# A recommender's attention scores: smaller pieces of the score table, placed all through the tile

## The chip, the core and the metric

The kernel runs on one core of one Trainium2 chip. The metric is the device time of one execution in microseconds (us), lower is better. A core has a matrix engine (PE; its weight loads are listed apart as PEld), a vector engine (DVE), a scalar engine (ACT), a general engine (POOL) and a queue that only issues transfers (SP). ACT and POOL issue transfers too. Each engine runs its own instructions in order and waits on semaphores for the others.

## The reference

For each of 2048 users there is a history of 200 items. An item is three ids below 1000, each with an embedding of 32 numbers; `ub` holds the histories' embeddings, `q` the embedding of the user's candidate item.

```python
att_in = jnp.concatenate([q, ub, q - ub, q * ub], axis=-1)
h = att_in @ w_att1.T + b_att1
score = (h @ w_att2.T + b_att2)[..., 0]
score = jnp.where(mask, 0.0, score)          # mask: first id is 0
browse = jnp.einsum('bl,ble->be', score, ub)
feat = jnp.concatenate([item_emb, browse, user_emb], axis=-1)
x = _dice(feat @ w1.T + b1, a1, g1, be1)     # normalised over the batch
x = _dice(x @ w2.T + b2, a2, g2, be2)
return jax.nn.sigmoid(x @ w3.T + b3)[:, 0]
```

Both layers in front of the score are linear, so for one user the score of a history item is a sum of three table values, one per id.

## The kernel before

**Work.** The 2048 users are 16 tiles of 128. A tile has 16 steps of 8 users, a step has two slots of 4 users, so a tile has 32 slots. An id is split in a high digit (40 values) and a low digit (25 values).

**Per tile.** PE multiplies the embedding tables with the tile's queries (L568) and gets all 3000 scores of each user. To keep full precision in bf16 the result is split in three parts: ACT copies the first (L761), PE subtracts it (L561), ACT copies the next, and so on. This is the splitting: 7 groups of low digits by 3 parts, one per slot, in slots 7 to 27 of the tile *before* the one that it is for. It writes `scores_b` (score values by table row on the partitions).

**Placement.** `place_scores` (L328) copies `scores_b` to `scoretab` by three transfers, one per id, of 40 partitions each. `scoretab` holds 128 users. The pieces are 16, 16, 32, 32, 32 users. Since the splitting of a tile ends in slot 27, the five pieces go out at its end: piece 0 and 1 in step 14, piece 2 in step 15, pieces 3 and 4 in steps 0 and 1 of the next tile. The next splitting, from slot 7 on, overwrites the one `scores_b`, so ACT waits for all five first (L893).

**Per step n.** DVE compares the high digits with 1 to 40 (`onehot_hi`, L967, for step n + 2), and SP turns the result around by a transposing transfer (`turn_hi`, L324, to `hiT`). In slot s PE multiplies `hiT` with the slot's part of `scoretab` (`read_scores`, L532), which needs the landed transfer and room in `sel` (two slots). DVE reduces `sel` (`pick`, L999) to scores, POOL splits them in three bf16 parts in six small operations (L431 to L444), DVE multiplies them with the one-hot of the low digits (`scale`, L1011), and PE adds them up with `onehot_hi` (`add_scores`, L549), 5 slots behind the reading. ACT copies the sums out (L754) and issues their transfers to `weightsum` (L830).

**DVE's order in a step**: pick(2n), `onehot_hi` of step n + 2, `onehot_lo` (L985), pick(2n + 1), in six steps of a tile a small piece of the digits, then scale(n - 1). `onehot_hi` waits until PE's sums have freed a slot of its ring.

**Unevenly spread work.** PE has the splitting in slots 7 to 27 and "finish" (L637, 25 fp32 products) in slots 9 to 15. POOL issues indirect gathers of item rows in steps 1 and 2 (L409) and of user rows in step 3 (L417). SP issues, in order: the transposes, the placements, a load of ids (`raw`, L315) in steps 2 and 9, and a store in step 11.

**Loops.** DVE, ACT, POOL and SP loop over tiles 1 to 14, one tile per pass. PE's loop holds seven tiles and is passed twice.

**The end.** Behind the last tile two batch-normalised layers run on buffers that reuse `scores_b` and `scoretab` (`x1`, `gate1`, `norm1`).

## Time and profile before

| | |
|---|---|
| median of 3 runs | 1591.98 us (1587.96 to 1605.28) |
| the profiled execution | 1586.62 us, span 1584.8 us |
| DVE busy | 1438.4 us (91%) |
| PE busy | 1328.5 us (84%) |
| POOL busy | 1131.4 us (71%) |
| ACT busy | 717.1 us (45%) |
| TensorE clock granted, mean | 0.921 |
| moved by DMA | 194.21 MB, mean 123 GB/s |

The profile is of one execution. Busy time is the union of an engine's instructions; waits are gaps on an engine, put down to the instruction or transfer whose semaphore came last. Line numbers (L532) are those of the kernel before. Transfers are issued by an engine's queue (SPq, ACTq) and are carried by 16 DMA engines that all queues share; q1 holds what SP issues, q10 what ACT issues, q8 and q14 fetch instructions.

### The profile page before, as it was taken

The page shows a single profiled execution, that of the slowest core. Times are in us where ns is not written, and L with a number is a line of the kernel's source. Part 1 is how long each engine was busy: PE and PEld are TensorE (multiplying, and loading weights), DVE is VectorE, ACT ScalarE, POOL GpSimd, SP SyncE. Part 2 cuts the span into 40 slices and gives each one's busy share as a digit, 9 for nine tenths or more (in the row PEclk, how much of TensorE's full clock was granted, in tenths as well). Part 3 has the DMA queues.
Part 4 walks back from the last instruction along what each step waited for, and adds up shares of the span by engine and source line. Part 5 has one row for each costly group of instructions (what it writes and reads, how often), then busy time and mean ns, then how long its engine had stood idle before and what let it go on. Part 6 is the DMA issues. An engine that isn't in the chain of part 4 may idle for free.

```text
span 1584.8 us, 67332 instructions
## 1 busy us (share of the span) xinstructions
PE 1328.5 (84%) x26911; PEld 1224.4 (77%) x26911; DVE 1438.4 (91%) x1453; ACT 717.1 (45%) x1633; POOL 1131.4 (71%) x1669
## 2 busy tenths in 40 slices
PE   5687989889797988979788797888989798887965
PEld 4576878778796887869788797888879797787861
DVE  7799999999999898999989899898999999899955
ACT  5353544536354453525435353453535355352217
POOL 3588788787878787776766768587787878677830
PEclk8799999999899998999999899999999899898966
DMA  2778676675857686584676758567686856668730
GB/s 30 146 109 159 104 146 124 130 149 111 168 100 151 108 137 134 111 167 95 138 111 128 147 111 154 92 141 131 111 167 112 151 107 144 118 115 157 117 70 0
DMA packets 510281, 194.21 MB, mean 123 GB/s; under 512 B 484005, under 2 KB 491797, under 8 KB 510045
## 3 DMA queue, kind: packets, MB, share of 16 engines
q1 hardware_dynamic: 492454, 162.61, 57.2%
q10 hardware_dynamic: 15448, 26.51, 6.5%
q8 instruction: 221, 3.62, 0.9%
q0 software_dynamic: 2144, 1.36, 0.8%
q14 instruction: 14, 0.11, 0.0%
HBM read 8.45 MB, written 1.44 MB: 6 GB/s over the span
## 4 chain that ended last, share of the span: by engine, by line
POOL 58%; issue 24%; DVE 6%; PE 5%; DMA 2%; POOLq 2%; SPq 2%; ACT 1%; DVEq 0%; ACTq 0%
POOL score L431 16%; POOL score L436 13%; POOL score_r L440 10%; POOL parts L441 6%; POOL parts L444 6%; POOL parts L437 3%; POOL item_rows L409 2%; DMA hiT<-onehot_hi 2%; POOL user_rows L417 2%; PE sel L532 1%; DVE score_j L999 1%; DVE onehot_hi L967 1%; DVE scaled_lo L1011 1%; PE wsum_ps L549 1%; PE misc L637 1%
## 5 line engine op out<-in xcount | busy, mean ns | idle before, releaser
L532 PE MATMUL sel<-scoretab,hiT 128*128 128x75 bf16 x12288 | 560.3, 206 | 142.8 <-DMA hiT<-onehot_hi 116.8
L532 PEld LDWEIGHTS sel<-scoretab,hiT 128*128 128x128 bf16 x12288 | 521.3, 103 | 204.1 <-issue 147.2
L549 PE MATMUL wsum_ps<-scaled_lo,onehot_hi 100*128 100x75 bf16 x12288 | 554.3, 204 | 73.8 <-DVE scaled_lo L1011 73.7
L549 PEld LDWEIGHTS wsum_ps<-scaled_lo,onehot_hi 100*128 100x128 bf16 x12288 | 509.4, 102 | 89.9 <-DVE scaled_lo L1011 83.8
L1011 DVE TENSOR_TENSOR scaled_lo<-onehot_lo,parts 100x3744 bf16<-100x3744 bf16 x256 | 539.4, 2107 | 24.0 <-POOL parts L444 20.0
L754 ACT ACTIVATE wsum_ring<-wsum_ps 128x300 f32<-128x300 f32 x512 | 215.5, 421 | 674.7 <-PE wsum_ps L549 668.1
L431 POOL TENSOR_TENSOR score<-score_j 100x16 f32<-100x16 f32 x256 | 310.4, 1213 | 293.4 <-DVE score_j L999 292.6
L999 DVE TENSOR_REDUCE score_j<-sel 100x24 f32<-100x600 f32 x512 | 395.8, 773 | 34.7 <-PE sel L532 34.0
L967 DVE TENSOR_TENSOR onehot_hi<-digits,iota_hi 100x1920 bf16<-100x1920 bf16 x256 | 297.5, 1162 | 45.9 <-PE wsum_ps L549 45.4
L761 ACT ACTIVATE scores_b<-acc 128x512 bf16<-128x512 f32 (+1 forms) x318 | 256.1, 805 | 44.9 <-PE acc L568 23.7
L436 POOL TENSOR_TENSOR score<-score,score_j 100x16 f32<-100x16 f32 x256 | 229.7, 897 | 22.0
L985 DVE TENSOR_TENSOR onehot_lo<-digits,iota_lo 100x1248 bf16<-100x1248 bf16 x256 | 211.5, 826 | 0.0
L440 POOL TENSOR_TENSOR score_r<-score,parts 100x16 f32<-100x16 f32 x256 | 168.8, 659 | 20.0
L444 POOL TENSOR_TENSOR parts<-score_r,parts 100x32 bf16<-100x32 f32 x256 | 122.8, 480 | 20.1
L441 POOL TENSOR_TENSOR parts<-score,parts 100x32 bf16<-100x32 f32 x256 | 129.2, 505 | 0.0
L637 PE MATMUL misc<-weightsum,table_blk 128*96 128x128 f32 x800 | 113.4, 285 | 4.6 <-DMA weightsum<-wsum_ring 4.6
L568 PE MATMUL acc<-queryT,tableT 97*128 97x128 f32 x758 | 111.6, 289 | 0.0
L561 PE MATMUL acc<-scores_b,minus_identb 128*128 128x512 bf16 (+1 forms) x212 | 101.2, 477 | 0.1
L637 PEld LDWEIGHTS misc<-weightsum,table_blk 128*96 128x96 f32 x800 | 93.9, 168 | 4.8 <-issue 4.8
L409 POOL DMA_INDIRECT item_rows<-in_L_rec_table_i_dram,ids_now x51 | 81.6, 1599 | 20.5 <-POOL ids_now L403 12.5
L568 PEld LDWEIGHTS acc<-queryT,tableT 97*128 97x128 f32 x758 | 94.6, 194 | 0.0
L857 ACT ACTIVATE onehot_hi<-digits,centre 100x48 bf16<-100x48 bf16 x256 | 91.6, 358 | 0.0
(155 smaller groups left out, 663.5 us busy)
## 6 DMA issues: line engine op xcount, KB each, us to landing
scoretab<-scores_b SPq DMA_DIRECT2D x144, 187.5 KB
weightsum<-wsum_ring ACTq DMA_DIRECT2D x128, 125.0 KB
weightsum<-wsum_ring ACTq DMA_DIRECT2D x64, 150.0 KB
scoretab<-scores_b SPq DMA_DIRECT2D x96, 93.8 KB
raw<-in_r_rec_his_dram SPq DMA_DIRECT2D x32, 150.0 KB
hiT<-onehot_hi SPq DMA_TRANSPOSE x256, 4.5
x_rows<-x_tile SPq DMA_DIRECT2D x14, 100.0 KB
scores_b<-x_rows SPq DMA_DIRECT2D x1, 1400.0 KB
```

The source lines that it names most:

```text
L431: pool.tensor_tensor(score_2[:, :], score_j[:, p2, :, 0], score_j[:, p2, :, 1], ALU.add).then_inc(parts_step, 1)
L436: pool.tensor_tensor(score[:, :], score_2[:, :], third, ALU.add)
L440: pool.tensor_tensor(score_r[:, :], score[:, :], parts[:, p2, :, 0, 0], ALU.subtract)
L441: pool.tensor_tensor(parts[:, p2, :, 1, :], twice(score[:, :]), parts[:, p2, :, 0, :], ALU.subtract).then_inc(parts_step, 1)
L444: pool.tensor_tensor(parts[:, p2, :, 2, :], twice(score_r[:, :]), parts[:, p2, :, 1, :], ALU.subtract).then_inc(parts_ready, 1)
L532: mm = pe.matmul(sel[:, 2 * (s % 2) + q, (c % 4) * W:(c % 4 + 1) * W] .rearrange("p (j v) -> p j v", j=NF), hiT[0:HJ, s // 2 % 4, g * POSP ...
L549: mm = pe.matmul(wsum_ps[:, s % 2, b * W:(b + 1) * W].rearrange("p (j v) -> p j v", j=NF), hi_columns(ring_slot(n), g), scaled_lo[:, n % 2 ...
L637: mm = pe.matmul(misc[0:E, 0:TILE].rearrange("p (w b) -> p w b", w=4), table_blk[:, lo, :, :].rearrange("p j e -> p (j e)"), weightsum[0:H ...
L761: act.activation(scores_b[:, :, stage, slice(*ROUNDS[r])], split_bank(first, r), ACT.Copy).then_inc(split_copied, 1)
L967: dve.tensor_tensor(onehot_hi[0:POS, ring_slot(n), :, HB:].rearrange("p g (j v d) -> p g j v d", j=NF, d=2), digits[:, hb, 1, g0:g0 + PER, ...
L999: dve.tensor_reduce(score_j[:, n % 2, g0:g0 + 8, :].rearrange("p (q c) j -> p q (c j)", q=2), sel[0:POS, 2 * (s % 2):2 * (s % 2) + 2, 0:4 ...
L1011: ins = dve.tensor_tensor(scaled_lo[:, n % 2, :, :, :].rearrange("p q i (u d) -> p (q i) u d", d=2), onehot_lo[:, n % 2, :, :, :].rearrang ...
```

## The change

`scoretab` now holds 64 users in four parts of 16 (HELD, CHUNK). Each tile has eight pieces of 16 users instead of five of 16 or 32. Pieces 0 and 1 go out in steps 14 and 15 of the tile before, pieces 2 to 7 behind the transpose of steps 0, 2, 4, 6, 8 and 10. A piece waits until PE has read the slots of the piece four before it (`sel_full`). `scores_b` has two halves that alternate by tile (`odd`), so the splitting of the next tile no longer waits for this tile's placement. The splitting's slots stay.

For `odd` to be a constant, SP and ACT now loop over pairs of tiles, seven passes, and PE has no loop: its 16 tiles are written out. DVE and POOL keep their loops. At the start DVE clears half as much of `scoretab` and copies the same constant rows in 12 smaller pieces instead of 6. At the end `gate1` and `norm1` lie elsewhere.

```diff
+    CHUNK = 16
+    CHUNKS = TILE // CHUNK
+    HELD = 4
...
-        scoretab_flat = sb("scoretab", [128, 2 * NF * HALF * 3 * LO], BF16)
+        scoretab_flat = sb("scoretab", [128, HELD * NF * CHUNK * 3 * LO], BF16)
...
-        scores_flat = sb("scores_b", [HJ, TILE * 3 * LO], BF16)
+        scores_flat = sb("scores_b", [HJ, 2 * TILE * 3 * LO], BF16)
...
-        ROWS = (0, 16, 32, 64, 96, 128)
-        CHUNKS = len(ROWS) - 1
...
-            def place_scores(t, c):
+            def place_scores(t, c, odd):
-                await_ge(split_copied, SPLIT_DONE * (t + 1))
-                b0, b1 = ROWS[c], ROWS[c + 1]
-                if isinstance(t, int) and t == 0:
-                    sp.wait_ge(scoretab_zero, b0 // HALF + 1)
+                g = CHUNKS * t + c
+                if c == 0:
+                    await_ge(split_copied, SPLIT_DONE * (t + 1))
+                if isinstance(g, int) and g < HELD:
+                    sp.wait_ge(scoretab_zero, c // 2 + 1)
                 else:
-                    await_ge(sel_full, SLOTS * t - (SLOTS - b1 // 4))
+                    await_ge(sel_full, (CHUNK // 4) * (g - HELD + 1))
...
-            def tile(t, last=False):
+            def tile(t, odd, last=False):
                 for n in range(STEPS):
-                    if n == 14 and not last:
-                        place_scores(t + 1, 0)
+                    if n >= 14 and not last:
+                        place_scores(t + 1, n - 14, 1 - odd)
                     if n + AHEAD < STEPS:
                         turn_hi(t, n + AHEAD)
                     elif not last:
                         turn_hi(t + 1, n + AHEAD - STEPS)
-                    if n < 2:
-                        place_scores(t, 3 + n)
+                    if n % 2 == 0 and n // 2 + 2 < CHUNKS:
+                        place_scores(t, n // 2 + 2, odd)
                     if n in (2, 9) and not last:
                         load_rows(2 * t + 2 + n // 9)
...
-                    if n >= 14 and not last:
-                        place_scores(t + 1, n - 13)
...
-            with sp.Fori(1, TILES - 1) as t:
-                tile(t)
-            tile(TILES - 1, last=True)
+            with sp.Fori(0, TILES // 2 - 1) as pair:
+                for odd in (1, 0):
+                    tile(pair * 2 + (2 - odd), odd)
+            tile(TILES - 1, 1, last=True)
...
-            with pe.Fori(0, (TILES - 2) // RUN) as run:
-                for i in range(RUN):
-                    for s in range(SLOTS):
-                        slot(run * RUN + (i + 1), s)
+            for t in range(TILES):
+                for s in range(SLOTS):
+                    slot(t, s, t % 2, last=t == TILES - 1)
...
                     if r == 0 and stage == 0:
-                        for c in range(CHUNKS):
-                            act.wait_ge(scoretab_in[c], (t + 1) * (NF * 16))
+                        for q in range(HELD):
+                            act.wait_ge(scoretab_in[q], t * ((CHUNKS // HELD) * (NF * 16)))
...
-            for hb in range(2):
-                dve.memset(scoretab_flat[:, hb * W * 3 * HALF:(hb + 1) * W * 3 * HALF].bitcast(F32), 0.0
-                           ).then_inc(scoretab_clear, 1)
+            half = (HELD // 2) * NF * CHUNK * 3 * LO
+            for h in range(2):
+                dve.memset(scoretab_flat[:, h * half:(h + 1) * half].bitcast(F32), 0.0).then_inc(scoretab_clear, 1)
```

The SP queue at the head of its loop (steps 0 to 2 of a tile), before. ISA and REGISTER_ALU rows are waits and counts; a row x2 is the second and third id of a piece; 40x2400 is a piece of 32 users, 40x1200 one of 16.

```order
L324 DMA_TRANSPOSE hiT<-onehot_hi 128x16x112 [waits sel_full]
L284 ISA
L284 ISA [waits split_copied]
L340 DMA scoretab<-scores_b 40x2400 [waits sel_full]
L340 DMA scoretab<-scores_b 40x2400 x2
L284 REGISTER_ALU
L284 ISA [waits hi_ready,lo_rows_ready]
L324 DMA_TRANSPOSE hiT<-onehot_hi 128x16x112 [waits sel_full]
L340 DMA scoretab<-scores_b 40x2400 [waits split_copied,sel_full]
L340 DMA scoretab<-scores_b 40x2400 x2
```

The same place now:

```order
L324 DMA_TRANSPOSE hiT<-onehot_hi 128x16x112 [waits sel_full]
L284 ISA
L340 DMA scoretab<-scores_b 40x1200 [waits sel_full]
L340 DMA scoretab<-scores_b 40x1200 x2
L284 REGISTER_ALU
L284 ISA [waits hi_ready,lo_rows_ready]
L324 DMA_TRANSPOSE hiT<-onehot_hi 128x16x112 [waits sel_full]
L284 REGISTER_ALU
L284 ISA [waits hi_ready,lo_rows_ready]
L324 DMA_TRANSPOSE hiT<-onehot_hi 128x16x112 [waits sel_full]
```

Between the transposes of step 0 and step 1 a piece of 32 users has become one of 16, and the piece between those of step 1 and step 2 is gone. The next piece stands behind the third transpose, ahead of the load of ids.

The SP queue at the end of a tile (step 15), before:

```order
L284 REGISTER_ALU [waits split_copied]
L340 DMA scoretab<-scores_b 40x1200 [waits sel_full]
L340 DMA scoretab<-scores_b 40x1200 x2
L284 REGISTER_ALU
L284 ISA [waits hi_ready,lo_rows_ready]
L324 DMA_TRANSPOSE hiT<-onehot_hi 128x16x112 [waits sel_full]
L284 REGISTER_ALU [waits split_copied]
L340 DMA scoretab<-scores_b 40x2400 [waits sel_full]
L340 DMA scoretab<-scores_b 40x2400 x2
```

And now, from the same piece on to the jump of the loop:

```order
L284 ISA
L340 DMA scoretab<-scores_b 40x1200 [waits sel_full]
L340 DMA scoretab<-scores_b 40x1200 x2
L284 REGISTER_ALU
L284 ISA [waits hi_ready,lo_rows_ready]
L324 DMA_TRANSPOSE hiT<-onehot_hi 128x16x112 [waits sel_full]
L375 REGISTER_ALU
L375 COMPARE_AND_BRANCH
```

The piece of 32 users behind the last transpose of the tile is gone. Between its two jump instructions SP's loop has 75 rows before and 166 now; ACT's loop has 207 rows before and 412 now, as its pass covers two tiles.

DVE at the start, before:

```order
L1085 MEMSET scoretab 128x7200 x2
L1091 COPY scoretab<-far 8x64x25 [waits scoretab_clear,far_in]
L1091 COPY scoretab<-far 8x64x25 x5
L967 TENSOR_TENSOR onehot_hi<-digits,iota_hi 100x16x120 [waits task_copied,const_ready]
L967 TENSOR_TENSOR onehot_hi<-digits,iota_hi 100x16x120
```

And now:

```order
L1084 MEMSET scoretab 128x3600 x2
L1090 COPY scoretab<-far 8x16x25 [waits scoretab_clear,far_in]
L1090 COPY scoretab<-far 8x16x25 x11
L965 TENSOR_TENSOR onehot_hi<-digits,iota_hi 100x16x120 [waits task_copied,const_ready]
L965 TENSOR_TENSOR onehot_hi<-digits,iota_hi 100x16x120
```

The first `onehot_hi` still stands behind the clearing, which is half as long.

## Rows read from the trace of the kernel before

**Rows 1.** the page: span, then busy time (share of the span) and instructions

```profile
span 1584.8 us, 67332 instructions
...
PE 1328.5 (84%) x26911; PEld 1224.4 (77%) x26911; DVE 1438.4 (91%) x1453; ACT 717.1 (45%) x1633; POOL 1131.4 (71%) x1669
```

**Rows 2.** ACT L798, once per tile: duration, first and last start

```profile
L798 ACT ACTIVATE item_prev<-item_last x14: 309/310/311, 136.5 to 1338.5; 96x128 f32<-96x128 f32 x14
```

**Rows 3.** waits of DVE, 139.7 to 1435.7 us: total, times, longest

```profile
DVE onehot_hi L967 <- PE wsum_ps L549: 42.8, 53, 1.3
DVE score_j L999 <- PE sel L532: 19.4, 14, 2.5
DVE scaled_lo L1011 <- POOL parts L444: 18.4, 30, 1.1
```

**Rows 4.** waits of PE, the same stretch

```profile
PE sel L532 <- DMA hiT<-onehot_hi: 98.8, 72, 4.7
```

**Rows 5.** busy time in two tiles: us, each engine, PEclk, DMA share, GB/s

```profile
230.70:320.80 90.10, 81.04 (x1718) 75.75 (x1716) 86.44 (x88) 44.51 (x105) 71.99 (x103) 0.95 0.67 134
877.80:972.00 94.20, 82.52 (x1715) 76.82 (x1712) 86.52 (x87) 44.10 (x104) 67.81 (x103) 0.93 0.66 127
```

**Rows 6.** DVE in tile 2: busy, mean ns | idle before <-releasers

```profile
L1011 DVE TENSOR_TENSOR scaled_lo<-onehot_lo,parts 100x3744 bf16<-100x3744 bf16 x17 | 35.8, 2107 | 2.7 <-POOL parts L444 2.7
...
L967 DVE TENSOR_TENSOR onehot_hi<-digits,iota_hi 100x1920 bf16<-100x1920 bf16 x16 | 18.6, 1165 | 1.0 <-PE wsum_ps L549 1.0
```

**Rows 7.** DVE by line in tile 9

```profile
L1011 DVE TENSOR_TENSOR scaled_lo<-onehot_lo,parts 100x3744 bf16<-100x3744 bf16 x17 | 35.8, 2108 | 0.9 <-POOL parts L444 0.6 <-PE wsum_ps L549 0.3
L999 DVE TENSOR_REDUCE score_j<-sel 100x24 f32<-100x600 f32 x32 | 24.7, 773 | 2.5 <-PE sel L532 2.5
L967 DVE TENSOR_TENSOR onehot_hi<-digits,iota_hi 100x1920 bf16<-100x1920 bf16 x16 | 18.6, 1161 | 4.3 <-PE wsum_ps L549 4.3
```

**Rows 8.** timeline of the SP queue, around tile 9: start us, us, what xcount

```profile
871.42 2.27 SPq L340 DMA_DIRECT2D scoretab<-scores_b  x3
...
885.23 1.58 SPq L324 DMA_TRANSPOSE hiT<-onehot_hi  x1
887.00 3.12 SPq L340 DMA_DIRECT2D scoretab<-scores_b  x3
890.55 3.27 SPq L324 DMA_TRANSPOSE hiT<-onehot_hi  x1
894.20 0.89 SPq L315 DMA_DIRECT2D raw<-in_r_rec_his_dram  x1
```

**Rows 9.** timeline of PE in tile 9: [idle before <-releaser]

```profile
900.27 1.70 PE L532 MATMUL sel<-scoretab,hiT 128*128 128x75 bf16 x24 [4.58 <-DMA hiT<-onehot_hi]
```

**Rows 10.** busy time at a tile boundary and in the steps behind

```profile
868.00:894.00 26.00, 20.88 (x475) 19.84 (x472) 26.00 (x26) 9.38 (x26) 20.65 (x27) 0.87 0.82 183
900.00:930.00 30.00, 29.73 (x524) 27.66 (x525) 23.68 (x25) 13.10 (x31) 15.52 (x33) 0.92 0.40 76
```

**Rows 11.** timeline of POOL in tile 2: a gather of rows

```profile
257.04 2.15 POOL L417 DMA_INDIRECT user_rows<-in_L_rec_table_user_dram,ids_now  x1 [0.81 <-POOL ids_now L414]
```

**Rows 12.** DVE by line, 22 to 42 us

```profile
L1085 DVE MEMSET scoretab<- 128x7200 f32 x2 | 12.1, 6058 | 2.9 <-issue 2.9
```

**Rows 13.** timeline of all engines at the start of the loop

```profile
38.27 2.71 ACT L761 ACTIVATE scores_b<-sel 128x512 bf16<-128x512 f32 x4
...
45.21 5.04 SPq L340 DMA_DIRECT2D scoretab<-scores_b  x6
...
49.76 0.48 PE L532 MATMUL sel<-scoretab,hiT 128*128 128x75 bf16 x5 [12.65 <-DMA scoretab<-scores_b]
```

**Rows 14.** jump of PE (L698): ns min/median/max

```profile
L698 PEldq COMPARE_BRANCH  x2: 83/1988/3893, 777.2 to 1433.0; - x2
```

**Rows 15.** jump of ACT (L913)

```profile
L913 ACTq COMPARE_BRANCH  x14: 44/50/54, 226.9 to 1434.2; - x14
```

**Rows 16.** page part 3, DMA queues: packets, MB, share of 16 engines

```profile
q14 instruction: 14, 0.11, 0.0%
```

More of the change, by code:

```diff
@@ L181, in build @@
         scoretab_clear = sem("scoretab_clear")
-        scoretab_in = [sem(f"scoretab_in{c}") for c in range(5)]
+        scoretab_in = [sem(f"scoretab_in{q}") for q in range(HELD)]
         weightsum_in = sem("weightsum_in")
@@ L553, in add_scores, with split_piece @@
                 mm.then_inc(wsum_full, 1)
-            def split_piece(r, piece, copied, first=False):
+            def split_piece(r, piece, copied, odd, first=False):
                 o = split_bank(first, r)
@@ L560, in split_piece @@
                     await_ge(split_copied, copied)
-                    mm = pe.matmul(o, minus_identb[:, :], scores_b[:, :, piece - 1, l0:l1], start=False,
+                    mm = pe.matmul(o, minus_identb[:, :], scores_b[:, odd, :, piece - 1, l0:l1], start=False,
                                    stop=(piece == 2), skip_group_check=True)
@@ L654, in task, with slot @@
                     mm.then_inc(task_full, 1)
-            def slot(t, s, last=False):
+            def slot(t, s, odd, last=False):
                 read_scores(t, s)
@@ L693, in _ @@
                         pe.wait_ge(const_ready, 2)
-                    split_piece(r, stage if stage else "all", NR * (stage - 1) + r + 1 if stage else 0, first=True)
+                    split_piece(r, stage if stage else "all", NR * (stage - 1) + r + 1 if stage else 0, 0, first=True)
             pe.wait_ge(split_copied, 3 * NR)
-            for s in range(SLOTS):
-                slot(0, s)
-            with pe.Fori(0, (TILES - 2) // RUN) as run:
-                for i in range(RUN):
-                    for s in range(SLOTS):
-                        slot(run * RUN + (i + 1), s)
-            for s in range(SLOTS):
-                slot(TILES - 1, s, last=True)
+            for t in range(TILES):
+                for s in range(SLOTS):
+                    slot(t, s, t % 2, last=t == TILES - 1)
             for s in range(SLOTS - LAG, SLOTS):
@@ L756, in copy_sums, with split_copy @@
                                ).then_inc(wsum_copied, 1)
-            def split_copy(r, stage, full, first=False):
+            def split_copy(r, stage, full, odd, first=False):
                 act.wait_ge(split_full, full)
-                act.activation(scores_b[:, :, stage, slice(*ROUNDS[r])], split_bank(first, r), ACT.Copy
+                act.activation(scores_b[:, odd, :, stage, slice(*ROUNDS[r])], split_bank(first, r), ACT.Copy
                                ).then_inc(split_copied, 1)
@@ L858, in lo_rows, with slot @@
                 act.activation(rows[:, :, :, 1], low, ACT.Square, bias=centre[:, :]).then_inc(lo_rows_ready, 1)
-            def slot(t, s, last=False):
+            def slot(t, s, odd, last=False):
                 here = tasks_of(t)
@@ L909, in _ @@
                 for r in range(NR):
-                    split_copy(r, stage, NR * stage + r + 1, first=True)
+                    split_copy(r, stage, NR * stage + r + 1, 0, first=True)
             for s in range(SLOTS):
-                slot(0, s)
-            with act.Fori(1, TILES - 1) as t:
-                for s in range(SLOTS):
-                    slot(t, s)
+                slot(0, s, 0)
+            with act.Fori(0, TILES // 2 - 1) as pair:
+                for odd in (1, 0):
+                    for s in range(SLOTS):
+                        slot(pair * 2 + (2 - odd), s, odd)
             for s in range(SLOTS):
-                slot(TILES - 1, s, last=True)
+                slot(TILES - 1, s, 1, last=True)
             for s in range(SLOTS - LAG, SLOTS):
```

56 lines of the change are left out of this document (29 added, 27 removed).

## The prediction, made before the changed kernel was run

> **What bounds the kernel now.** I read the busy times first. DVE is busy for 91% of the span, PE for 84% [rows 1], so DVE is the likely bound and what can be won is DVE's idle time inside the loop. Next the pace: a line of ACT that runs once per tile starts first at 136.5 and last at 1338.5, 13 tiles apart, so a tile takes 92.5 us [rows 2]. DVE's own work in a tile is constant: 86.4 us in tile 2, which takes 90.1, and 86.5 in tile 9, which takes 94.2 [rows 5]. The rest, about 6 us a tile, is waiting. The waits over tiles 1 to 14 say for whom: 42.8 us for PE's sums, 19.4 for PE's products in `sel`, 18.4 for POOL's `parts` [rows 3]. That is 80.6 us in all, 5.8 a tile, and 62.2 of it for PE.
>
> PE in turn lost 98.8 us in the same stretch waiting for `hiT`, the transposed one-hots [rows 4]. So I looked at the queue that moves them. Around the tile boundary SP issues in turn a transpose (1.58 us) and a piece of the score table: 2.27 us for 16 users, 3.12 for 32 [rows 8]. The last one before the stall is issued at 887.00 and holds SP until 890.12. Then the transpose of step 4 starts at 890.55 and takes 3.27 us to issue, twice the normal. PE reaches the slot that needs it and stands idle for 4.58 us, until 900.27 [rows 9]. From there DVE first waits 2.5 us for `sel`, then 4.3 for sums, since the splitting and "finish" begin just then and PE, at work for 29.73 of the next 30 us, never gets its lead back [rows 7, 10]. The transfers are close to full at the boundary (DMA share 0.82, 183 GB/s) and half empty behind it (0.40, 76 GB/s) [rows 10]: placement is one burst of five pieces in a quiet-enough tile.
>
> Tile 2 shows the same kernel without a bad stall: there DVE waits 2.7 us for POOL and 1.0 for sums, and not at all for `sel` [rows 6]. In tile 9 the POOL share is 0.6, because DVE's other waits let POOL catch up [rows 7]. So POOL's lateness is a second limit right behind PE's. It comes from the gathers: one of them holds POOL for 2.15 us behind a wait of 0.81 [rows 11], and there are four a tile.
>
> **The change, part by part.** *Placement at the boundary.* The piece between the transposes of step 1 and step 2 of a tile goes, as does the one behind the last transpose of the tile before, and that behind the transpose of step 0 shrinks from 32 to 16 users. (Each transpose is for two steps later.) SP gains the 3.12 us that stood right ahead of the critical transpose, which can be issued when DVE has it ready, and finds the queue empty. I take it that PE's stall before slot 8 goes in most tiles, because both causes of that transpose's lateness, SP's time and the queue's, are gone.
>
> *Placement in the middle.* Pieces 3 to 7 now go out in steps 2 to 10. On SP a transpose and a piece take 1.58 + 2.27 = 3.85 us [rows 8], less than the 5.4 us of a step (86.5 / 16), and every second step has no piece, so lateness cannot add up. In these steps the DMA share was 0.40 [rows 10]. The piece that could hurt is piece 3, with the load of ids (0.89 us) behind it [rows 8], ahead of the transpose of step 5: 2.27 + 0.89 after the transpose of step 4. I price this below as a rival. The waits on `sel_full` look back four pieces, 16 slots, less than what the next transpose asks for anyway: nothing. Nine more issues a tile cost SP time that it has.
>
> *The loop's gain.* If PE's stall goes, a tile looks like tile 2, whose PE waits (1.0) stay at worst and whose POOL waits (2.7) stay in full, since nothing here touches POOL: 86.5 + 3.7 = 90.2. A little of the 1.0 should go as well, since even in tile 2 PE had late transposes; I take 90.1. From 92.5 that is 2.4 us a tile, 34 us over 14 tiles. At most DVE's waits for PE all go with POOL's no longer than now, 62 us, or with POOL's too, 80.6 [rows 3]; at least half of the wait for `sel` goes, 10 us.
>
> *The start.* DVE's two clearings of `scoretab` take 12.1 us [rows 12], now half: 6.0 less. The first `onehot_hi` and its transpose stand behind them, and SP's first placement at 45.21 behind those; PE's first product waits for it for 12.65 us, until 49.76. But the placement also needs the first splitting, whose last copies ACT ends at 38.27 + 2.71 = 41.0 [rows 13]. So it can start 45.2 - 41.2 = 4 us sooner: 4 gained, between 0 and 6.
>
> *Tiles 0 and 15.* They have a boundary each, outside the 14 counted: 2 us together, between 0 and 5.
>
> *ACT's wait* for the placement ahead of the splitting and the second half of `scores_b`: ACT is at 45%, nothing. *The end*: the same work elsewhere in memory, nothing.
>
> *Loops.* PE's jump back, executed once, took 3893 ns; its loop holds seven tiles and must be fetched again. That jump goes; some 1 us of it reached DVE. ACT's 14 jumps took at most 54 ns [rows 14, 15], and the fetching queue of the small engines moved only 14 packets in the whole span [rows 16], so their bodies stay on the chip over the passes. ACT's body grows from 207 to 412 rows, SP's from 75 to 166. If ACT's no longer stays, each pass has a jump of up to 3.9 us; it lies at the end of slot 31, where ACT is ahead of its work. I charge 3 us for the 7 passes, between 0 and 27.
>
> The Trainium skill, "Runtime: NRT & Kernel Launch", section "Instruction fetch mechanics", says that a taken branch to code outside a window of two pages forces a fetch before execution goes on, and that this is why full unrolling is often preferred. PE's row agrees with it, ACT's short jumps too; by it the doubled bodies speak against this change, PE's unrolling for it.
>
> **Sum.** Against the profiled execution's 1586.6: - 34 - 4 - 2 - 1 + 3 = - 38, so 1548.6. The median of the runs shown is 5.4 above the profiled one, the lowest 1.4 above; I add 2 and say **1550 us**.
>
> **Rivals.**
> - *PE's and POOL's waits both go.* A tile falls to 87 to 88, near DVE's 86.5. For it: POOL's small operations get no slower, and with PE ahead its sums never delay DVE. Against: tile 2 shows POOL's waits growing when PE's go. 5 us x 14 = 70, with the rest 74: 1512 to 1515.
> - *The stall moves one step on.* The transpose of step 5 now lands behind piece 3, the load of ids and POOL's gathers, just where PE's heavy part starts. For it: 2.27 + 0.89 us are ahead of it on SP. Against: they are less than a step. PE's lead is lost again and only 0.5 to 1 us a tile is won: 7 to 14 us, with the start 11 to 18, so 1570 to 1577.
> - *Nothing moves but the start.* The stalls would come from something else, such as the granted clock, which is 0.87 around the boundary and 0.92 behind it [rows 10]; tile 2 has 0.95 and tile 9 0.93 [rows 5]. Against: 0.02 of PE's 81 us is under 2 us, and PE's stall is plainly for `hiT`. About 1586.
> - *Slower: code is fetched in each pass.* ACT's body of 412 rows is fetched page by page behind each jump, and SP's too; SP carries the transposes, which have no slack at the boundary. At 3.9 us a fetch, four fetches a pass, 7 passes: 109 us, about 1655. It decides from 8 us a pass that reach DVE (1608 less 1550, over 7). Against: PE streams 27,000 products [rows 1] through such fetches and pays only at the jump, so one fetch a pass is likelier than four.
>
> **Chances.** Forecast (a tile at 89 to 91) 0.64; both waits go 0.10; the stall moves 0.15; nothing moves 0.06; slower by fetching 0.05. A measurement of this kernel can tell about 1%, 16 us: faster is below 1576, slower above 1608. Faster: 0.64 + 0.10 + half of the moved stall = 0.82. Same: the other half and "nothing" = 0.13. Slower 0.05. The range leaves out the fetching, "nothing", and the lower half of the second case: 1518 to 1577.
>
> **What would show it.** Right: PE's wait for `hiT` falls from 98.8 us to under 50 in the loop; DVE's waits for `sel` nearly vanish and those for sums fall to 10 to 20 us, while those for POOL's `parts` grow from 18 to some 35; tiles come every 90 us and nearly alike; DMA share is level over the tile; the first product starts near 46. Wrong: gaps of PE for `hiT` remain in step 4 or 5, waits for `parts` do not grow, jumps of ACT or SP take microseconds, or the fetching queue has hundreds of packets.

## The result and the profile after

| | before | changed |
|---|---|---|
| median | 1593.57 us (4 runs, 1587.96 to 1605.28) | 1529.37 us (4 runs, 1528.07 to 1531.98) |
| profiled execution, span | 1586.62, 1584.8 | 1528.07, 1525.9 |
| busy: DVE, PE, POOL | 91%, 84%, 71% | 94%, 85%, 77% |

The ratio is 0.959, with a 95% interval of 0.9534 to 0.9646. That is 64 us less by the medians and 58.6 by the profiled executions. The prediction said 1550.

The page of the changed kernel, its part 1, answers to [rows 1]:

```profile
span 1525.9 us, 65969 instructions
...
PE 1295.6 (85%) x26911; PEld 1182.9 (78%) x26911; DVE 1427.4 (94%) x1459; ACT 716.0 (47%) x1633; POOL 1172.3 (77%) x1669
```

DVE has nearly the same work in a shorter span: 1427.4 us where it was 1438.4. Of the 11 us less, 6.9 lie ahead of its first reduction (the clearing is 6.0 of them) and 3.6 in tiles 1 to 14. PE's busy time fell from 1328.5 to 1295.6 us with the same 26,911 products. The granted TensorE clock rose from 0.921 to 0.955 in the mean, so PE spent less time at the lower of its two levels. POOL's busy time rose, from 1131.4 to 1172.3 us, with the same 1669 instructions: the last operation that makes `parts` (L444) takes 566 ns in the mean where it took 480, the second (L436) 939 for 897, and a gather of user rows 2217 for 1663. Why they got longer is open.

The line of ACT that runs once per tile (L794 now, duration, first and last start), against [rows 2]:

```profile
L794 ACT ACTIVATE item_prev<-item_last x14: 309/310/312, 131.6 to 1290.8; 96x128 f32<-96x128 f32 x14
```

13 tiles take 1159.2 us, 89.2 each, where it was 92.5. They are also alike: cut at DVE's first reduction, tiles 1 to 14 take 89.03 to 89.26 us. Before they took 89.79 to 94.87.

The waits of DVE and of PE over the same 14 tiles (134.7 to 1381.9 us; total, times, longest), against [rows 3, 4]:

```profile
DVE scaled_lo L1009 <- POOL parts L444: 26.5, 36, 1.1
DVE scaled_lo L1009 <- PE wsum_ps L550: 10.6, 19, 1.1
DVE onehot_hi L965 <- PE wsum_ps L550: 0.6, 2, 0.4
```

```profile
PE wsum_ps L550 <- DVE scaled_lo L1009: 93.5, 105, 1.4
PE sel L533 <- DMA hiT<-onehot_hi: 29.5, 36, 1.9
```

PE's wait for `hiT` fell from 98.8 to 29.5 us. DVE's wait for `sel` (19.4) is gone, and the one of `onehot_hi` for sums fell from 42.8 to 0.6. The wait for `parts` grew from 18.4 to 26.5, and the scaling now waits 10.6 us for sums. In all DVE idles 37.7 us in the 14 tiles, where it was 81.8. (In the kernel before that is the 80.6 us of [rows 3] and 1.2 us of the scaling waiting for sums.) What is left of PE's wait for `hiT` lies mostly in steps 0, 3, 12 and 15 (23.0 of the 29.5 us), and none of it makes DVE wait for `sel`.

Tile 2 by line (busy, mean ns, idle before), against [rows 6]:

```profile
L1009 DVE TENSOR_TENSOR scaled_lo<-onehot_lo,parts 100x3744 bf16<-100x3744 bf16 x17 | 35.8, 2106 | 2.7 <-POOL parts L444 2.7
...
L965 DVE TENSOR_TENSOR onehot_hi<-digits,iota_hi 100x1920 bf16<-100x1920 bf16 x16 | 18.6, 1164 | 0.0
```

The 1.0 us of waiting for sums is gone, the 2.7 for POOL are the same to a tenth. Every tile is now the old tile 2 without its waits for PE.

The SP queue around tile 9 (start, us; a merged row spans its waits), against [rows 8]:

```profile
838.45 2.02 SPq L324 DMA_TRANSPOSE hiT<-onehot_hi  x1
840.67 2.25 SPq L340 DMA_DIRECT2D scoretab<-scores_b  x3
844.14 6.76 SPq L324 DMA_TRANSPOSE hiT<-onehot_hi  x2
851.12 2.89 SPq L340 DMA_DIRECT2D scoretab<-scores_b  x3
854.64 7.00 SPq L324 DMA_TRANSPOSE hiT<-onehot_hi  x2
861.84 2.36 SPq L340 DMA_DIRECT2D scoretab<-scores_b  x3
864.59 0.37 SPq L315 DMA_DIRECT2D raw<-in_r_rec_his_dram  x1
865.37 7.15 SPq L324 DMA_TRANSPOSE hiT<-onehot_hi  x2
```

Between the transposes of steps 1 and 2 nothing is issued any more: two transposes share the row at 854.64, the second of them the one that was late. The next piece goes out at 861.84, behind it.

Busy time and DMA share at the same boundary and in the steps behind it, against [rows 10]:

```profile
837.00:863.00 26.00, 19.94 (x477) 18.95 (x473) 26.00 (x27) 9.38 (x26) 20.57 (x28) 0.93 0.65 144
869.00:899.00 30.00, 29.74 (x570) 27.10 (x571) 28.25 (x30) 14.33 (x33) 23.50 (x37) 1.00 0.63 120
```

The share is 0.65 and 0.63 where it was 0.82 and 0.40: the same bytes (194.4 MB in all, 194.2 before), now level. The granted clock went from 0.87 to 0.93 at the boundary and from 0.92 to 1.00 behind it.

At the start, the clearing by line and the first product, against [rows 12, 13]:

```profile
L1084 DVE MEMSET scoretab<- 128x3600 f32 x2 | 6.1, 3058 | 1.4 <-issue 1.4
```

```profile
41.67 4.59 SPq L340 DMA_DIRECT2D scoretab<-scores_b  x6
...
45.86 1.68 PE L533 MATMUL sel<-scoretab,hiT 128*128 128x75 bf16 x24 [8.06 <-DMA scoretab<-scores_b]
```

The first placement starts at 41.67 instead of 45.21, right behind ACT's last copy of the first splitting (38.97 to 41.65), and the first product at 45.86 instead of 49.76.

### The profile page after: what moved, and what is told of

Same layout as the page of the kernel before. It is cut to its first block, busy times and chain, and to the rows that moved or that the text cites. A ratio compares the mean times of both kernels' runs of the same rounds, so it can differ in the third digit from the quotient of the medians.

```text
span 1525.9 us, 65969 instructions
## 1 busy us (share of the span) xinstructions
PE 1295.6 (85%) x26911; PEld 1182.9 (78%) x26911; DVE 1427.4 (94%) x1459; ACT 716.0 (47%) x1633; POOL 1172.3 (77%) x1669
## 4 chain that ended last, share of the span: by engine, by line
POOL 67%; issue 19%; PE 4%; DVE 3%; POOLq 2%; ACT 2%; DMA 1%; ACTq 1%; SPq 0%; DVEq 0%
POOL score L431 18%; POOL score L436 15%; POOL score_r L440 10%; POOL parts L444 8%; POOL parts L441 7%; POOL parts L437 4%; POOL item_rows L409 2%; POOL user_rows L417 2%; DVE score_j L997 1%; DMA hiT<-onehot_hi 1%; DVE onehot_lo L983 1%; PE misc L638 1%; PE sel L533 1%; ACT scores_b L757 1%; PE wsum_ps L550 1%
## 5 line engine op out<-in xcount | busy, mean ns | idle before, releaser
L550 PE MATMUL wsum_ps<-scaled_lo,onehot_hi 100*128 100x75 bf16 x12288 | 534.7, 201 | 117.7 <-DVE scaled_lo L1009 117.1
L533 PEld LDWEIGHTS sel<-scoretab,hiT 128*128 128x128 bf16 x12288 | 499.2, 100 | 131.1 <-DMA hiT<-onehot_hi 51.6
L550 PEld LDWEIGHTS wsum_ps<-scaled_lo,onehot_hi 100*128 100x128 bf16 x12288 | 487.6, 99 | 141.8 <-DVE scaled_lo L1009 137.5
L533 PE MATMUL sel<-scoretab,hiT 128*128 128x75 bf16 x12288 | 537.5, 202 | 69.0 <-DMA hiT<-onehot_hi 38.7
L436 POOL TENSOR_TENSOR score<-score,score_j 100x16 f32<-100x16 f32 x256 | 240.3, 939 | 22.0
L444 POOL TENSOR_TENSOR parts<-score_r,parts 100x32 bf16<-100x32 f32 x256 | 144.8, 566 | 20.1
L854 ACT ACTIVATE onehot_hi<-digits,centre 100x48 bf16<-100x48 bf16 x256 | 91.7, 358 | 0.0
```

Source lines behind the costliest of these rows:

```text
L436: pool.tensor_tensor(score[:, :], score_2[:, :], third, ALU.add)
L444: pool.tensor_tensor(parts[:, p2, :, 2, :], twice(score_r[:, :]), parts[:, p2, :, 1, :], ALU.subtract).then_inc(parts_ready, 1)
L533: mm = pe.matmul(sel[:, 2 * (s % 2) + q, (c % 4) * W:(c % 4 + 1) * W] .rearrange("p (j v) -> p j v", j=NF), hiT[0:HJ, s // 2 % 4, g * POSP ...
L550: mm = pe.matmul(wsum_ps[:, s % 2, b * W:(b + 1) * W].rearrange("p (j v) -> p j v", j=NF), hi_columns(ring_slot(n), g), scaled_lo[:, n % 2 ...
```

## The experiments

Each ratio is to the kernel before, timed beside it; the median of that was 1596.36 us for e1, e3, e4 and e7, 1596.12 for e2, e5, e6 and e8, and 1591.34 for e9 to e12. So medians of different groups carry some 5 us of doubt. Steps are counted from 0 and, where their length is given, cut at DVE's first reduction of each.

| run | median us | ratio, 95% interval |
|---|---|---|
| e1, whole burst again | 1581.06 | 0.9941 (0.9904 to 0.9978) |
| e7, 32 users at step 1 | 1578.15 | 0.9878 (0.9804 to 0.9952) |
| e12, 16 users at step 1 | 1550.56 | 0.9753 (0.9704 to 0.9801) |
| e4, piece 3 at step 1 | 1531.63 | 0.9608 (0.9551 to 0.9665) |
| e3, pieces of 32 | 1542.29 | 0.9702 (0.9627 to 0.9777) |
| e2, before, PE in one pass | 1583.96 | 0.9933 (0.9894 to 0.9972) |
| e6, no pair loops | 1527.70 | 0.9601 (0.9535 to 0.9667) |
| e5, gathers spread | 1520.92 | 0.9569 (0.9501 to 0.9638) |
| e8, before, gathers spread | 1591.24 | 1.0016 (0.9973 to 1.0058) |
| e9, gathers and ids spread | 1523.47 | 0.9575 (0.9528 to 0.9622) |
| e10, and x1 in pieces | 1518.51 | 0.9551 (0.9499 to 0.9603) |
| e11, and finish from slot 8 | 1520.83 | 0.9548 (0.9500 to 0.9597) |

### Was it the burst at the boundary?

The theory: transfers of the score table ahead of the transposes made these late, and the last one, in step 1, decided. The rivals: the freed wait on `scores_b`, PE's written-out code, the memory layout, or only the size of a piece.

**e1_burst_again.** The changed kernel with the old traffic put back at the boundary. Pieces 2 and 3 go out as one behind the transpose of step 0 (`place_pair`). The copies to a spare buffer compute nothing; the two halves and the loops stay.

```diff
+            def extra(done, odd):
+
+                if not (isinstance(done, int) and done == 0):
+                    await_ge(spare_in, done * (NF * 16))
+                for j in range(NF):
+                    r = slice(hi_first(j), hi_first(j) + HI)
+                    sp.dma_start(spare[r, :], scores_b[r, odd, 2 * CHUNK:4 * CHUNK, :, :].rearrange("p b k v -> p (b k v)")
+                                 ).then_inc(spare_in, 16)
...
-                    if n % 2 == 0 and n // 2 + 2 < CHUNKS:
+                    if n == 0:
+                        place_pair(t, odd, False)
+                    if n == 1:
+                        extra(t * 2, odd)
+                    if n == 15 and not last:
+                        extra(t * 2 + 1, 1 - odd)
+                    if n % 2 == 0 and 4 <= n // 2 + 2 < CHUNKS:
                         place_scores(t, n // 2 + 2, odd)
```

> The changed kernel with the old traffic at the tile boundary put back: behind the transpose of step 0 a piece of 32 users (pieces 2 and 3 together), behind those of steps 1 and 15 a copy of 32 users' size to a spare buffer. Everything else (two halves of scores_b, smaller table, loops) is as in the changed kernel. If the burst was what delayed the transposes, most of the 48 us that the loop won come back: tiles of 91 to 93 us instead of 89.1, 1560 to 1590 us, and DVE waits for sel and for PE's sums return. If the gain came from the freed wait on scores_b, from PE's written-out code or from memory layout, it stays within 10 us of 1529.

Measured: 1581.06 us. 52 of the 64 us are back by the medians (0.035 of 0.041 by the ratios), though the kernel keeps everything else of the change, and its tiles 1 to 14 take 91.7 us in the mean. The profiled execution, at 1570.61 us, is the fastest of its ten. Its waits from 134.7 to 1381.9 us (the 14 tiles of the changed kernel; in this and the next runs that stretch ends within the last of them):

```profile
DVE onehot_hi L1002 <- PE wsum_ps L585: 35.6, 44, 1.3
...
DVE score_j L1034 <- PE sel L568: 13.5, 10, 3.8
```

```profile
PE sel L568 <- DMA hiT<-onehot_hi: 86.7, 67, 6.0
```

As the first expectation has it, DVE waits for `sel` and for sums again, and PE's wait for `hiT` is back near the 98.8 of before. The run moves more than the kernel before, since the copies come on top of a tile's full 128 users. But the loss lies where the old one lay: step 3 takes 6.82 us in the mean and step 8 6.45 (before 7.22 and 6.47, in the changed kernel 5.92 and 5.31), and steps 9 to 15 are as in the changed kernel.

So the second half of `scores_b`, the loops and the layout carry little themselves: 9 us by the ratio (4 to 15 by its interval) are left for them together, of which the start is 4. The second half is still needed, as with one half the splitting, from slot 7 on, would have to wait for pieces that go out up to step 10. Whether a table of 128 users beside two halves would do as well was not tried.

**e7_one_piece_at_step_1.** The same without the copy in step 15 (the edit is shown against e1).

```diff
-                    if n == 15 and not last:
-                        extra(t * 2 + 1, 1 - odd)
```

> As the one with the whole burst, but without the copy in step 15: 32 users behind the transpose of step 0 and 32 users' size behind that of step 1. If the one issue of 3.1 us right ahead of the transpose of step 4 decides (what the prediction said), this costs nearly as much as the whole burst: over 1555 us. If lateness builds up over the whole boundary, it costs half or less of it: 1535 to 1550 us.

Measured: 1578.15 us, 49 above the changed kernel and well over the 1555 of the first expectation; the piece in step 15 adds nothing that can be told apart (the intervals of e1 and e7 overlap, and e7's profiled execution is the slowest of its four, 1585.35). The loss is made by what stands in steps 0 and 1.

```profile
DVE onehot_hi L1000 <- PE wsum_ps L583: 39.5, 50, 1.3
...
DVE score_j L1032 <- PE sel L566: 18.8, 8, 5.2
```

```profile
PE sel L566 <- DMA hiT<-onehot_hi: 94.2, 67, 7.3
```

**e12_pieces_of_16_twice.** The same with 16 users' size in step 1 (32 stay behind step 0; the edit is shown against e7).

```diff
-        spare = sb("spare", [HJ, 2 * CHUNK * 3 * LO], BF16)
+        spare = sb("spare", [HJ, CHUNK * 3 * LO], BF16)
...
-                    sp.dma_start(spare[r, :], scores_b[r, odd, 2 * CHUNK:4 * CHUNK, :, :].rearrange("p b k v -> p (b k v)")
+                    sp.dma_start(spare[r, :], scores_b[r, odd, 2 * CHUNK:3 * CHUNK, :, :].rearrange("p b k v -> p (b k v)")
```

> Between two runs done: 32 users behind the transpose of step 0 and 16 users' size (to a spare buffer) behind that of step 1. 16 and 16 cost 2 us, 32 and 32 cost 49. If the size right ahead of the transpose of step 4 decides, it stays near 16 and 16: 1530 to 1540 us. If the sum over the boundary decides, it lies half-way: 1545 to 1560 us.

Measured: 1550.56 us, 21 above the changed kernel.

**e4_piece_3_at_step_1.** No extra copies; piece 3 alone moves one step forward, ahead of the transpose of step 4.

```diff
-                    if n % 2 == 0 and n // 2 + 2 < CHUNKS:
-                        place_scores(t, n // 2 + 2, odd)
+                    if n == 1 or n % 2 == 0 and n // 2 + 2 < CHUNKS and n != 2:
+                        place_scores(t, 3 if n == 1 else n // 2 + 2, odd)
```

> The changed kernel with piece 3 (16 users) one step earlier, ahead of the transpose of step 4 instead of behind it. Of the changed kernel's slack this takes 2.3 us of SP just there. If the transposes at the boundary have no slack, 5 to 20 us slower than 1529; if the stall of before needed the pieces of 32 users, within 3 us of it.

Measured: 1531.63 us, 2 above the changed kernel, and its four runs (1529.88 to 1534.35) overlap those of the changed kernel. That is the expectation for a stall that needed the pieces of 32 users.

Put in a row by users placed behind the transposes of steps 0 and 1: 16 and 0 takes 1529, 16 and 16 1532, 32 and 16 1551, 32 and 32 1578. The cost does not grow evenly. The first 16 users in step 1 are nearly free, and each 16 more cost 19 and then 28 us by the medians; by the ratios, which allow for the two groups of runs, it is 3, 23 and 20 us. So whether the price still rises beyond 32 users is open. That fits a queue with some slack, not one fixed price per piece, and both steps count: e12's expectation "half-way" held, not the one that only the size right ahead decides.

The traces also say what makes the critical transpose late. These are the two pieces of 32 users ahead of the one of 3.12 us in [rows 8]:

```profile
876.52 2.50 SPq L340 DMA_DIRECT2D scoretab<-scores_b  x3
881.92 2.55 SPq L340 DMA_DIRECT2D scoretab<-scores_b  x3
```

So size alone costs SP little: a piece of 16 takes 2.3 to 2.4 us in the changed kernel, one of 32 2.3 to 2.9 in e3, below (medians by place), and 3.1 only at the critical place of the kernel before. The transpose for step 4 is issued some 0.3 us behind its `onehot_hi` in the changed kernel and e4, and 1.0, 1.0 and 1.5 us behind in e12, e7 and the kernel before (medians over tiles 1 to 14). Its own issue takes 1.6 and 1.9 us in the first two, and 2.1, 3.1 and 3.0 in the others. The transpose for step 3, for which the traces have the landing, lands 3.8 us after the start of its issue in the changed kernel, 5.1 in e4, 6.2 in e12, 5.8 in e7 and 6.2 before. So holding SP makes up about 1.2 us of the lateness, and the rest is that the transposes themselves are slower behind the larger pieces. No run separates the two by an edit, such as placing from another queue.

**e3_pieces_of_32.** Pieces of 32, but apart: in step 14 and behind the transposes of steps 0, 4 and 8. The table still holds 64 users.

```diff
-    CHUNK = 16
+    CHUNK = 32
...
-    HELD = 4
+    HELD = 2
...
-                    if n % 2 == 0 and n // 2 + 2 < CHUNKS:
-                        place_scores(t, n // 2 + 2, odd)
+                    if n in (0, 4, 8):
+                        place_scores(t, n // 4 + 1, odd)
```

> The changed kernel with four pieces of 32 users, a table of two parts of 32 (the same 64 users), placed in step 14 of the tile before and behind the transposes of steps 0, 4 and 8. If what counts is that the pieces lie apart, within 5 us of 1529. If what counts is that a piece is small (3.1 against 2.3 us of SP, and half the bytes ahead of a transpose), 10 us or more slower, with PE waiting for hiT behind steps 0, 4 and 8.

Measured: 1542.29 us, 13 above the changed kernel (by the ratios 18), which meets the second expectation, 10 us or more. The waits, from 134.7 to 1381.9 us:

```profile
DVE score_j L996 <- PE sel L532: 7.2, 13, 1.0
```

```profile
PE sel L532 <- DMA hiT<-onehot_hi: 54.2, 41, 2.9
```

PE waits 54.2 us for `hiT` where it was 29.5, mostly in steps 0, 3, 11 and 12, and DVE 7.2 for `sel`, in steps 0, 11 and 12. So of the 64 us, 13 to 18 come from halving the pieces, and the rest, 46 to 51, from pulling the burst apart, together with the start's 4. As SP's time for a piece is nearly the same in both sizes, "3.1 against 2.3 us of SP" is hardly the reason, which leaves the bytes ahead of a transpose.

### Did the loops matter?

**e2_pe_one_pass.** The kernel before, with `RUN = 14` instead of 7: PE's loop is passed once.

```diff
-        RUN = 7
+        RUN = 14
```

> The kernel before with PE's loop of 14 tiles in one pass instead of 7 in two, so that its jump of 3.9 us is gone and nothing else. The prediction's share for this: 1 us, so within 5 us of before. If PE's code layout were behind the gain of the change, 10 us or more faster.

Measured: 1583.96 us against 1596.12, ratio 0.9933 (0.9894 to 0.9972). The medians are 12 us apart, the profiled spans only 1.6 (1583.2 against 1584.8), and DVE's tiles 1 to 14 take 92.5 us in the mean, the 92.6 of before. By the medians this is the expectation for PE's code layout, 10 us or more, and not the one of within 5; by the profiles it is the other. So the size is open: 4 to 17 us by the interval, 1 to 2 by the profiles. The kernel before itself ranges over 1577 to 1603 us in the runs beside the experiments, and its profiled execution, at 1586.62, lies at the low end of that. The waits say that the cause of the main gain is untouched: PE still waits 93.6 us for `hiT` in the 14 tiles, where it was 98.8. But what e1 kept, 9 us by the ratio, can in part be this.

**e6_no_pair_loops.** The changed kernel with SP's and ACT's loops written out (SP's is shown).

```diff
-            with sp.Fori(0, TILES // 2 - 1) as pair:
-                for odd in (1, 0):
-                    tile(pair * 2 + (2 - odd), odd)
+            for t in range(1, TILES - 1):
+                tile(t, t % 2)
```

> The changed kernel with SP's and ACT's loops over pairs written out, so neither jumps. The queue that fetches their code moved 53 packets in the changed kernel, 14 before. If fetching behind the jumps reaches DVE, 2 to 20 us are won; if it is hidden, as the even tiles of 89.06 us suggest, within 3 us of 1529.

Measured: 1527.70 us, 1.7 less. The page's row of the queue that fetches code, in the changed kernel and in this one, against [rows 16], and ACT's jump in the changed kernel against [rows 15]:

```profile
q14 instruction: 53, 0.43, 0.1%
```

```profile
q14 instruction: 33, 0.27, 0.1%
```

```profile
L910 ACTq COMPARE_BRANCH  x7: 48/54/54, 308.8 to 1377.9; - x7
```

The pair loops do fetch code again: 53 packets, while SP and ACT written out take 33. The jump instruction itself takes 54 ns at most, but ACT stands still behind it: its next instruction starts 2.4 to 3.7 us later in each of the six passes that jump back, where it was 0.2 us in the kernel before. So in the changed kernel's timeline of ACT, behind the jump at 486.9 us:

```profile
490.75 0.31 ACT L794 ACTIVATE item_prev<-item_last 96x128 f32<-96x128 f32 x1 [3.54 <-issue]
```

SP goes on 0.3 us behind its jump, as before. PE waits for ACT's `item_now` behind three of the jumps, 3.1 us in all, but nothing of this reaches DVE: the tiles take 89.09 us with the pair loops and 89.04 without.

### What bounds it now?

**e5_gathers_spread.** In the changed kernel POOL's item gathers move from steps 1, 2, 2 to 6, 9, 13.

```diff
-                if n == 1 and not last:
+                if n == 6 and not last:
                     await_ge(task_full, task_before(t, 0) + 1)
-                    copy_item_ids(t + 2, 2 * t + 3)
+                    copy_item_ids(t + 2, 2 * t + 4)
                     gather_items((0,))
-                if n == 2 and not last:
-                    gather_items((1, 2))
+                if n == 9 and not last:
+                    gather_items((1,))
+                if n == 13 and not last:
+                    gather_items((2,))
...
-                    gather_users(t, 2 * t + (3 if last else 4))
+                    gather_users(t, 2 * t + 3)
```

> The changed kernel with POOL's three gathers of item rows moved from steps 1, 2 and 2 to steps 6, 9 and 13; the one of user rows stays in step 3. If POOL's lateness behind the gathers is the limit that is left (28.0 us of DVE waiting for parts, 42.0 of all idle time ahead of the scaling), DVE gets 1.5 to 2.4 us a tile back: tiles of 86.7 to 87.6 us, 1495 to 1508 us. If DVE or PE is the limit anyway, within 5 us of 1529.

Measured: 1520.92 us, 8.5 less instead of 21 to 34.

```profile
DVE scaled_lo L1011 <- POOL parts L444: 18.4, 23, 1.1
DVE onehot_hi L967 <- PE wsum_ps L552: 11.5, 16, 1.2
DVE scaled_lo L1011 <- PE wsum_ps L552: 1.5, 5, 0.3
```

The waits ahead of the scaling in steps 3 and 4 went, under both names (for `parts` and for sums), the one of step 5 stayed (1.12 us a tile), and `onehot_hi` waits 11.5 us for PE's sums, mostly in step 8, where there was 0.6. PE's sums are a third limit. That its heavy slots make them late is argued only.

**e8_before_gathers_spread.** The same edit in the kernel before.

> The kernel before with the same move of the gathers. There PE's stall for the transposes comes first and gives POOL time to catch up, so if the two limits lie one behind the other, less is won than in the changed kernel: 0 to 18 us (the 18.4 us of waits for parts), 1575 to 1593 us. If they add, as much as there: 25 to 34 us.

Measured: 1591.24 us, ratio 1.0016 (0.9973 to 1.0058): nothing. Its waits over the 14 tiles (139.7 to 1435.7 us), against [rows 3]:

```profile
DVE onehot_hi L969 <- PE wsum_ps L551: 48.0, 69, 1.3
DVE score_j L1001 <- PE sel L534: 21.4, 21, 2.9
DVE scaled_lo L1013 <- POOL parts L444: 7.4, 11, 1.1
```

11 us of waiting for POOL went, and 7.2 of them came back as waits for PE. While PE's stall stands first, POOL's gathers are nearly free.

**e9_gathers_and_ids_spread.** SP and ACT without loops, the user gather in step 6 with its ids copied in step 4, item gathers in 9, 12 and 13 with ids copied in step 8.

```diff
+                if n == 4:
+                    copy_user_ids(t)
+                if n == 6:
+                    gather_users(t, 2 * t + 3)
+                if n == 8 and not last:
+                    copy_item_ids(t + 2, None)
+                if n == 9 and not last:
+                    await_ge(ids_ready, 2 * t + 4)
+                    gather_items((0,))
+                if n == 12 and not last:
+                    gather_items((1,))
+                if n == 13 and not last:
+                    gather_items((2,))
```

> The changed kernel with no loops on SP and ACT, and POOL's work spread further: user ids copied in step 4, gathered in 6; item ids copied in step 8, gathers in 9, 12 and 13. With only the item gathers moved, DVE still waited 1.12 us a tile for parts in step 5 and newly 0.75 us for PE's sums in step 8. If the lone user gather with its copy in step 3 causes the 1.12, that goes: tiles near 87.5 us, 1500 to 1510 us. If PE takes it over in step 8, little is won: 1515 to 1521 us.

Measured: 1523.47 us, no better than e5, and 2 us above even the second expectation.

```profile
DVE onehot_hi L972 <- PE wsum_ps L558: 19.5, 24, 1.3
DVE scaled_lo L1016 <- POOL parts L446: 12.1, 27, 0.6
```

The wait for `parts` in step 5 fell from 15.7 us over the 14 tiles to 4.1, so the lone user gather was its cause; 8.0 of the 12.1 us now stand in step 11. PE's sums rose to 19.5 us, 14.3 of them in step 8: what POOL gives up PE takes.

**e10_x1_in_pieces.** As e9, with the load of x1 in the last tile in seven pieces, in steps 3 to 9 instead of one in step 11.

```diff
-                    if n == 11 and last:
+                    if n == 3 and last:
...
+                    if 3 <= n < 10 and last:
+                        piece = slice((n - 3) * 2 * TILE, (n - 2) * 2 * TILE)
+                        sp.dma_start(x1[:, :, piece], x1_rows[:, :, piece]).then_inc(x1_in, 16)
```

> As the one with ids and gathers spread, and the load of x1 in the last tile (1400 KB in one transfer in step 11) in seven pieces in steps 3 to 9. The last tile's step 13 takes 7.87 us against 5.21 of its neighbours in the changed kernel. If that is the same thing, a transpose behind a large transfer on its queue, 2 to 3 us are won against the kernel without this edit; if not, nothing.

Measured: 1518.51 us, the lowest median of the study, 5 us below e9 and 11 below the changed one, though the intervals to before of e5, e9, e10 and e11 overlap, and so do the runs of e9 and e10. The last tile in the changed kernel, PE's waits and DVE's timeline:

```profile
PE sel L533 <- DMA hiT<-onehot_hi: 5.0, 1, 5.0
```

```profile
1453.57 2.09 DVE L1009 TENSOR_TENSOR scaled_lo<-onehot_lo,parts 100x3744 bf16<-100x3744 bf16 x1
1458.23 0.78 DVE L997 TENSOR_REDUCE score_j<-sel 100x24 f32<-100x600 f32 x1 [2.58 <-PE sel L533]
```

One transpose behind a transfer of 1400 KB on its queue makes PE wait 5.0 us and DVE 2.58, then 1.54 more for its next product. In e10 step 13 takes 5.21 us, like its neighbours, against 7.87 in the changed kernel and 8.60 in e9: the same mechanism at a second place. But part of the stall moved to the pieces. PE waits 3.54 us for a transpose in step 10, and steps 10 and 11 take 6.43 and 6.02 us, where they took 5.91 and 5.21 in e9:

```profile
1430.65 1.70 PE L543 MATMUL sel<-scoretab,hiT 128*128 128x75 bf16 x24 [3.54 <-DMA hiT<-onehot_hi]
```

Up to its last reduction the last tile takes 81.4 us, and 85.0 in e9.

**e11_finish_in_8_slots.** As e10, with PE's "finish" in slots 8 to 15.

```diff
-        PARTS = 7
-        FIN_SLOT = 9
+        PARTS = 8
+        FIN_SLOT = 8
```

> As the one with x1 in pieces, and PE's finish products (25 of fp32) in slots 8 to 15 instead of 9 to 15. If PE's load in slots 9 to 15 is the limit that is left behind POOL's, DVE's wait for sums in step 8 shrinks by half or more: 3 to 8 us faster. If PE then has to wait for weightsum in slot 8, it is slower.

Measured: 1520.83 us, nothing won. DVE's wait for sums in step 8 stayed at 1.0 us a tile, so one more slot for "finish" is not what it lacks. Whether the splitting's slots matter was not tried.

## Why the prediction was right, and where its sizes were off

**What bounds: right.** PE's stall for `hiT` at the tile boundary was the cause, and DVE's waits for PE followed from it. e1 shows it from the other side: the traffic back, 52 of 64 us back. That the piece right ahead of the critical transpose decides held with a limit: e7 against e1 shows that step 15 does not count, but e12 against e4 that the piece in step 0 counts as well. Of the two causes named, "SP's time and the queue's", SP's was the smaller by the traces, some 1.2 us. And the 3.12 us are not the price of 32 users, which take 2.50 and 2.55 in the two rows ahead: they belong to that crowded place.

**Placement in the middle: right.** Pieces 3 to 7 cost nothing that shows: DVE has no wait for `sel` in the 14 tiles. The rival that the stall moves to the transpose of step 5 did not come true: steps 5 to 8 of a tile take 6.65, 5.69, 5.69 and 5.31 us in the mean, and before 6.53, 6.06, 6.09 and 6.47.

**The loop's gain: the term was too small.** I gave 2.4 us a tile and 34 in all; it was 3.5 us (92.57 to 89.09) and 48.8. The failing step was "whose PE waits (1.0) stay at worst ... I take 90.1": I kept 0.9 of the 1.0 that tile 2 waited for sums. Tile 2 had late transposes too, only less so, and its waits for PE went wholly. 86.4 of work and the 2.7 of waits that had stood under POOL's name are 89.1, what every tile takes. 15 of the 21 us of the miss lie here.

**POOL as the next limit: right in kind.** The 2.7 us of tile 2 were a good forecast of every tile. The total of waits for `parts`, 26.5 us, is below the "some 35", but with the scaling's waits for PE's sums (10.6) it is 37.1. The two names hardly differ there: in e6, with the same pace, the same 37.1 us are 17.4 and 19.7, and e5 takes from both at once. e5 and e9 show that POOL's limit and that of PE's sums lie close together: freeing POOL further gave nothing. And the rival's premise that POOL's small operations get no slower did not hold (1131.4 to 1172.3 us busy).

**The start: right, for the reason given.** 3.9 us (49.76 to 45.86) for 4: the placement now waits for ACT's last copy, which ends at 41.65.

**Tiles 0 and 15: too small.** 5.0 us for 2: from the first reduction of each tile, tile 0 takes 87.1 instead of 88.2, and tile 15 83.5 instead of 87.4 up to the last reduction. 2.7 us of that are in step 3 of tile 15, the boundary stall.

**Loops: the stall right, its price on the safe side.** 3 us were charged for fetching code and 1 given for PE's jump. ACT's body of 412 rows did not stay on the chip: ACT stands still for 2.4 to 3.7 us behind each of its six jumps back, near the "up to 3.9 us" of the prediction, and where it said, at a place where ACT is ahead. e6 says that at most 1.7 us of all this reach the time. The sign "jumps of ACT or SP take microseconds" would have missed it, since the jump's own row says 54 ns and the stall stands as idle time behind it. The slower rival failed because there was one such stall a pass and not four, none on SP, and none reached DVE. The Trainium skill, "Runtime: NRT & Kernel Launch", section "Instruction fetch mechanics", says that a taken branch to code outside the window of two pages waits for a fetch before it goes on. The trace agrees for ACT (53 packets where it was 14, and the 2.4 to 3.7 us), and has no such stall for SP.

**From the profiled execution to the median.** 2 us were added; it was 1.3 (1529.37 less 1528.07), against 7.0 for the kernel before with its fourth run. So the misses did not cancel: nearly all of them are on the side of too little.

**The clock** was set aside as a cause, rightly as far as the runs go: it follows the stalls. In e1, with only the transfers changed and the same products, the mean granted clock of its runs is 0.922 to 0.934, where the four of the changed kernel have 0.951 to 0.958. How much of a stall's price is the lower clock behind it is not separated.

## What to carry to other kernels

Where short, urgent transfers and bulk transfers share one queue, spread the bulk in small pieces behind the urgent ones, with twice buffered sources to allow it: here the same bytes at a level DMA share of 0.65 kept DVE from no product, and in a burst, at 0.82, they cost some 50 us. Look at how long the urgent transfer itself takes, and not only at how long the queue is held ahead of it. Take the pace of the kernel's own best stretch as the forecast for a removed stall, and treat waits in that stretch for the same engine as gone too; the wait for another engine stays. Then look at the second and third limit before promising more: spreading POOL's gathers gave nothing while the first stall stood and 8.5 of a hoped 21 to 34 us after it. And look for the price of a jump in the idle time behind it, not in its own row.

## What the runs showed that I had not expected

The cost of late transposes is uneven. Behind steps 0 and 1 together, 16, 32, 48 and 64 users gave 1529, 1532, 1551 and 1578 us: nearly free up to 32, then some 20 to 28 us for each 16 more. With the stall gone the runs also agree better: 1528 to 1532 us over 4 runs, where the 4 of the kernel before beside them spread over 1588 to 1605. And a loop body whose code is fetched anew (53 packets against 33 written out) held ACT for 2.4 to 3.7 us in each pass and cost the kernel next to nothing.
